# The scan layer of a six-layer network: the output product in three pieces, the value product in two, and the transposition in another PSUM bank

## The reference, cut to what matters

```python
q = (x @ W_q.T); k = (x @ W_k.T); v = x @ W_v.T      # x is layer-normed, q and k in 8 heads of 64
b = (q * k).sum(-1) * SCALE
a = -softplus(x @ W_alpha_w.T + W_alpha_b).sum(-1)
vs, vl = sign(v), log(abs(v) + EPS)
def step(carry, inp):                                # once for each of the 63 later tokens
    ln, nm, sg = carry
    ln = stable_lse(a_t + ln, b_t)
    m = max(a_t + nm, b_t + vl_t)
    ssum = sg * exp(a_t + nm - m) + vs_t * exp(b_t + vl_t - m)
    nsg, nm = sign(ssum), m + log(abs(ssum) + EPS)
    y = (nsg * exp(nm - ln)).sum(over heads)
y @ W_o.T                                            # added to x
```

## Time and profile before

| | |
|---|---|
| time, median of 3 runs (lowest, highest) | 2039.79 us (2038.75, 2043.52) |
| the profiled execution's own time | 2044.84 us |
| its span | 2042.4 us |
| busy, whole span | PE 92%, PEld 74%, DVE 65%, ACT 55%, POOL 7% |
| the scan's eight groups | about 1543 to 1811 us of the span |
| in the scan's stretch 1545 to 1815 | PE 244.25 us busy, DVE 247.27, ACT 182.55, of 270 |

### The profile page before, as it was taken

One profiled execution on the slowest core, in us unless ns is written; L12 is line 12 of the kernel. 1 busy time (PEld: TensorE's weight loads), 2 busy tenths in 40 slices (PEclk: granted clock), 3 DMA queues, 4 the chain that ended last, 5 costly groups with the idle time before them and its releaser, 6 DMA issues. The chain is left out here.

```text
span 2042.4 us, 31431 instructions
## 1 busy us (share of the span) xinstructions
PE 1881.7 (92%) x10506; PEld 1501.4 (74%) x10506; DVE 1333.6 (65%) x2451; ACT 1124.4 (55%) x1864; POOL 136.6 (7%) x130
## 2 busy tenths in 40 slices
PE   7989985999997599999999999999968899889998
PEld 4667875999996578787878787878746667665664
DVE  4784546999996474636363545454528898878686
ACT  5762324888885354545454444444426666656663
POOL 0001000111110110000000000000000000002221
PEclk9999976999999799999999999999987988879999
DMA  6300042453424221101010101012040000020000
GB/s 235 108 32 1 1 161 90 150 205 128 178 89 165 93 71 34 51 16 51 15 51 15 51 15 51 15 51 82 16 141 42 1 1 1 1 88 1 1 21 21
DMA packets 22750, 129.80 MB, mean 64 GB/s; under 512 B 3601, under 2 KB 3857, under 8 KB 18962
## 3 DMA queue, kind: packets, MB, share of 16 engines
q1 hardware_dynamic: 17714, 112.59, 15.0%
q0 software_dynamic: 4960, 16.26, 2.4%
HBM read 116.51 MB, written 12.32 MB: 63 GB/s over the span
## 5 line engine op out<-in xcount | busy, mean ns | idle before, releaser
L116 PE MATMUL PS<-cT,qs 128*128 128x512 f32 x1152 | 298.4, 404 | 3.3 <-DVE qs L1697 2.2
L116 PE MATMUL PS<-pT,cN 128*128 128x512 f32 x1152 | 269.8, 392 | 1.7 <-DVE pT L1697 1.7
L116 PEld LDWEIGHTS PS<-cT,qs 128*128 128x128 f32 x1152 | 209.5, 188 | 52.6 <-issue 8.9
L116 PEld LDWEIGHTS PS<-pT,cN 128*128 128x128 f32 x1152 | 213.9, 188 | 45.0 <-DVE pT L1697 1.9
L116 PE MATMUL PS<-fw,xgT 128*128 128x384 f32 x1104 | 204.6, 340 | 5.7 <-DVE xgT L1244 5.7
L116 PEld LDWEIGHTS PS<-fw,xgT 128*128 128x128 f32 x1104 | 193.3, 190 | 9.3 <-DVE xgT L1244 6.3
L1692 DVE TENSOR_REDUCE nmax<-PS 128x1 f32<-128x512 f32 x128 | 87.8, 686 | 156.5 <-PE PS L116 156.4
L1244 DVE TENSOR_TENSOR fw<-W,fw 128x1536 fp32r<-128x1536 f32 x92 | 159.4, 1755 | 22.8 <-ACT fw L1164 22.8
L116 PE MATMUL PS<-xT,ws 128*128 128x512 f32 x576 | 155.1, 422 | 15.1 <-PEq L2599 8.7
L1597 ACT ACTIVATE qp<-PS 128x512 f32<-128x512 f32 x96 | 57.4, 598 | 187.9 <-PE PS L116 187.9
L1164 ACT ACTIVATE fw<-W 128x1536 fp32r x92 | 134.4, 1488 | 33.2 <-issue 33.2
(11 more groups left out here) (289 smaller groups left out, 3406.8 us busy)
## 6 DMA issues: line engine op xcount, KB each, us to landing
W<-in_fc SPq DMA_DIRECT2D x8, 3072.0 KB, 11.0
cT<-in_ctxT SPq DMA_DIRECT2D x16, 768.0 KB, 4.3
raw_pj<-in_proj SPq DMA_DIRECT2D x8, 1536.0 KB
ct_in<-in_ctxT SPq DMA_DIRECT2D x16, 768.0 KB, 4.3
cn_in<-in_ctxN SPq DMA_DIRECT2D x16, 768.0 KB
W<-in_w SPq DMA_DIRECT2D x2, 4096.0 KB, 13.1
routed_y<-y POOLq DMA_DIRECT2D x22, 256.0 KB
W<-in_w SPq DMA_DIRECT2D x5, 1024.0 KB, 7.1
```

The source lines that it names most:

```text
L116: mm = nc.tensor.matmul(out, lhs(m, s), rhs(n, s), start=(opens and (s, m, n) == terms[0]), stop=((s, m, n) == terms[-1]))
```

## The change

The output product of group c - 1 no longer stands as four matmuls at j = 5. Two of them stand at j = 3, one at j = 4 and one at j = 5, behind whatever the branch on j gives and ahead of `head_sums`. The value product of group c + 2 no longer stands as twelve matmuls at j = 7: six stand at j = 6 and six at j = 7. The transposition writes into ps[0] in place of ps[3]; it waits for `take_q` of the group before (the last reader of ps[0]) in place of `add_out`, and the output product's wait for the turned tile is gone. Number and shape of the matmuls are unchanged, and so are the programs of DVE, ACT, POOL and SP, but for the bank that the two readers of the turned tile read.

```diff
+    OUT_AT = {3: range(0, 2), 4: range(2, 3), 5: range(3, DK)}
...
-        ln = Norm(nc, e, "5", sbuf, ps[3], xT[0])
+        ln = Norm(nc, e, "5", sbuf, ps[0], xT[0])
...
-                def project(c, w):
+                def project(c, w, ks=range(DK)):
...
-                    split_product(nc, bank, lambda part, k: xT[c % 2][part][:, k, :],
-                                  lambda part, k: ws[part][:, ORDER.index(w), k, :], DK, w != W5_A).then_inc(done, 1)
+                    n = ORDER.index(w)
+                    for k in ks:
+                        for m, r in ((0, 0), (0, 1), (1, 0)):
+                            mm = nc.tensor.matmul(bank, xT[c % 2][m][:, k, :], ws[r][:, n, k, :],
+                                                  start=(k == 0 and m == r and w != W5_A),
+                                                  stop=(k == DK - 1 and m == 1))
+                    if ks[-1] == DK - 1:
+                        mm.then_inc(done, 1)
...
-                def out_proj(c):
+                def out_proj(c, ks=range(DK)):
...
-                    pe.wait_ge(ln.xT_ready, BASE + min(c + 4, NG))
                     pe.wait_ge(z_used, BASE + c)
-                    for k in range(DK):
+                    for k in ks:
                         mm = nc.tensor.matmul(ps[3], yT[:, c % 2, k, :], wo[:, k, :], start=(k == 0), stop=(k == DK - 1))
-                    mm.then_inc(z_mm, 1)
+                    if ks[-1] == DK - 1:
+                        mm.then_inc(z_mm, 1)
...
-                    pe.wait_ge(z_used, BASE + max(c - 3, 0))
+                    pe.wait_ge(q_sb, BASE + c)
                     ln.tensor(pe, c)
...
-                        elif j == 5 and c >= 1:
-                            out_proj(c - 1)
+                        elif j == 6 and c + 2 < NG:
+                            project(c + 2, W5_V, range(0, 2))
                         elif j == 7 and c + 2 < NG:
-                            project(c + 2, W5_V)
+                            project(c + 2, W5_V, range(2, DK))
+                        if c >= 1 and j in OUT_AT:
+                            out_proj(c - 1, OUT_AT[j])
                         head_sums(t)
```

## The result

The changed kernel takes 2050.38 us (median of 6 runs, 2047.38 to 2052.93) against 2040.84 us of the kernel before (6 runs): a ratio of 1.0046, 95% interval 1.0033 to 1.0059. It is 9.5 us slower. In a second job its median was 2051.23 (5 runs), ratio 1.0037 (1.0024 to 1.0050). A ratio here is the recorded estimate from the runs of both kernels in one job; it can differ from the quotient of the two medians by a little over 0.1%. The prediction said 2036.3, with 2044.5 as the upper end of its range, and gave "slower by over 0.3%" a chance of 0.08; the fourth case, with 2048, comes nearest.

The account below looks back on a forecast made before the run. DVE's program was taken to set the scan's pace, with at most 17.9 us of its waits to win. The terms 4.2 - 1.4 + 0.3 + 0.4 gave 3.5 us less, 2036.3 us, with an 8-in-10 range of 2028.5 to 2044.5.

Parts of the forecast that it names:

- the fourth case: Rival: small pieces no longer bring the clock up, steps 6 and 7 run at 1.2 GHz; 2048 us, chance 0.10.
- What bounds the scan: In the scan DVE's program sets the pace; at most its 17.9 us of waits, 15.2 for ACT's ear, can be won.
- end minus 5.32: DVE's wait for ear is the decay product's end, counted from DVE's step 0, minus 5.32, to within 0.07 in four groups.
- The output product in the free time of steps 3 and 4: Cut in pieces, most of it fits PE's free time around steps 3 and 4; with the value halves, 4.2 us gained.
- the value halves: Value product halved over steps 6 and 7: last `head_sums` has half a product less ahead, lateness near zero in groups 3 to 6.
- debt: The output product at step 5 works 5.00 us, past DVE's start of step 6; steps 6 and 7 carry that on.
- lateness: Start of the old group's last `head_sums` after DVE's step 0; expected near zero in groups 3 to 6.
- The clock of the decay product: Slow decay products, partly at the low clock, go from three of six to four of six; taken as -1.4 us.
- The banks: `turn_x` waiting for `take_q` and the new bank's other waits pass in PE's free time; counted 0.
- the product of keys: DVE waits 1.9 us for it in six groups; bounds 0 and 1.9, gain taken 0.3 us.
- the last output product: DVE's 0.8 us wait in `add_out` of group 7 should go; bounds 0 and 0.8, gain taken 0.4 us.
- The base: Profiled execution of 2044.84 us, taken to stay 5.05 above the runs' median 2039.79, from which 3.5 us was taken.

Follow-up runs that it names:

- e1: Changed kernel with the value product put back whole at step 7, output product still in pieces at steps 3, 4, 5: 2054.03 us, 1.0047 of the kernel before.
- e5: Changed kernel with the output product as one block at step 3 and the value product whole at step 7: 2055.19 us, 1.0058 of the kernel before.
- e15: Output product cut in halves at steps 5 and 6, value product whole at step 7: 2043.44 us, 1.0010 of the kernel before.
- e4: Changed kernel plus nine unused matmuls in every group but the last, three at step 4, six at step 5: 2043.18 us, 1.0006 of the kernel before.
- e6: Output product whole at step 4, value product in halves at steps 6 and 7: 2047.15 us, 1.0032 of the kernel before.
- e2: Changed kernel with the output product put back whole at step 5, value product still in halves: 2038.73 us, 0.9977 of the kernel before.
- e3: Changed kernel with both products put back whole, only the transposition's bank and its waits changed: 2041.54 us, 1.0000 of the kernel before.

## Why the prediction was wrong

- *What bounds the scan*: right. DVE's waits for ear, the end of the decay product and the line "end minus 5.32" held in the changed kernel too: in groups 1 to 5 of both its profiles it gives the wait to within 0.12 us (4.35 forecast by it in group 3 of the first, 4.28 found).
- *The output product in the free time of steps 3 and 4, worth with the value halves 4.2 us*: this is the step that failed. The pieces went where the text said and the pauses shrank. But the sum took the block at step 5 for mere debt, and put the price of its leaving, which the fourth case names, at nothing. With the block there, the clock was down in step 5 and up for steps 6 and 7 (0.50 and 0.96 in group 3); with pieces at steps 3 to 5 it was up in step 5, where a pause of 2 us opened, and down for steps 6 and 7 (1.00 and 0.50). So lateness, in place of going to zero, went from 0.0 to 1.6 us in groups 2 to 6 up to 2.2 to 2.6 us in three of these in one profile and in four in the other. e1 and e5 (the product or most of it at steps 3 and 4: 2054 and 2055), e15 (at steps 5 and 6: 2043) and e4 (clock held up by filling: on time) show it. e6 sets its limit: a block at step 4 left PE on time. What makes the clock fall in one group and not in the next of the same code stays open.
- *The fourth case* was this mechanism, with a chance of 0.10. Its trigger was put wrongly: "small pieces no longer bring the clock up". A block at step 3 does no better. Its price was near: 3.84 us late was worked out, 2.2 to 2.6 was measured in the groups that are late. It was too high by the adding up: the sum laid the lengths of six items end to end, 11.4 us, while in group 2 of the first profile they overlap and take 10.35 us from start to start (1635.80 to 1646.15), and the first of them starts 0.20 us ahead of DVE's step 6. "It decides from two groups on" held: the second profile has five late by over 2 us.
- *The value halves*: right in sign. e2 gains 0.23%. The text placed the gain in lateness near zero; e2's products are late by about 1 us in groups 1 to 5, and five of its six are fast.
- *The clock of the decay product, four of six slow*: right as a count. It is slow in groups 2, 3, 5 and 6 of the first profile and in 1, 3, 4 and 5 of the second. It was meant for a PE that is on time; where PE is (e4, e6) it is slow in five and in four of six, at the most one more than counted. The reading behind it was too short: the clock of group 3 before did not fall behind the 1.57 us pause but within it (0.60 as its mean over the pause), and another pause, of 1.78 us, stood ahead of the `head_sums` of step 3, which the text left out. The row of that `head_sums`, and the stretch of the later pause:

```profile
1665.23 1.06 PE L1936 MATMUL PS<-cn,W 128*128 128x16 f32 x8 [1.78 <-DVE W L2248]
```
```profile
1667.07:1668.64 1.57, 0.00 (x2) 0.00 (x1) 1.57 (x6) 0.77 (x2) 0.00 (x0) 0.60 0.00 0
```

- *The banks, the product of keys, the last output product*: 0 for the banks is confirmed by e3 (1.0000); keys 2.0 us after 1.9, so 0 and not 0.3; the 0.8 went.
- *The base*: I read one profile as the kernel. e3, of the same time, has a scan 4.8 us shorter and waits 10.5 us for ear, not 15.2, so part of the waits that I counted as to be won were that execution's.

Of the two rules of the Trainium skill ("TensorE: Matmul & The Clock Gate"), the one in "Why this matters for your kernels", that dense work without long gaps keeps the clock, agrees with e4, whose steps 5 to 7 ran at 1.00. It does not tell where the clock falls here: the longest pause of PE for DVE in the scan was 2.2 us before and 2.3 us in the changed kernel, and the clock fell in both. The other rule of the Trainium skill, on small pauses, in "A second HAM failure mode: psum-queue depth-cycling", spoke against cutting; here e15, cut, was within 0.1% of the kernel before, and the place mattered more.

## What to carry to other kernels

When an engine waits in one step and is late in another, a block of work between them may decide which of the later steps run at the low clock; before moving it into the earlier pause, look at the granted clock step by step, and at which steps can bear the low one. Give each part of a change a run of its own: here a loss of 0.5% covered a gain of 0.2%. Starting a product whose end sets the pace earlier in part (the decay halves) can help, but it is no rule: here it helped with the output block at step 4 and hurt with it at step 5.

## What the runs showed of the hardware

Adding 63 matmuls of 512 columns to PE, for results nobody reads, made the kernel 7 us faster (2043.2 against 2050.4 and 2051.2): the granted clock of steps 5 to 7 in group 3 went from 0.69 to 1.00. PE was busy by the profile for 10 of 12.3 us in both. Executions of one kernel spread by up to 12 us (e1: 2045.8 to 2058.1), more than those of the kernel before (2036.6 to 2045.6 in the same job), and the same group waits differently in two profiles of one kernel: group 1 of the changed kernel waited 1.5 us for ear in the first and 4.9 in the second.
